# Two key blocks' weights of the first head pair made between the roots, with two table loads more

## The reference

```python
# _cdist: d2 = q2[..., :, None] + k2[..., None, :] - 2.0 * qk;  sqrt(max(d2, 0))
P = layernorm(x) @ W_in + b_in            # 16 heads x (Q, K, V, G), 64 wide each
W = jnp.power(EPS + _cdist(Q, K), -P_POW)  # EPS 1e-4, P_POW 2
W = W / (EPS + jnp.sum(W, axis=-1, keepdims=True))
A = jnp.einsum('hbts,hbse->hbte', W, V)
H = G * A                                  # then H @ W_out + b_out
```

## Time and profile before

| of the profiled execution | |
|---|---|
| its own time | 1395.16 us |
| span, first to last instruction | 1393.3 us |
| TensorE matmul busy | 1254.6 us (90%) |
| VectorE busy | 1129.7 us (81%) |
| ScalarE busy | 1034.0 us (74%) |
| GpSimd busy | 678.8 us (49%) |
| start, to the first distances of pair 1 | 74.4 us |
| granted TensorE clock, mean | 0.96 of full |

### The profile page before, as it was taken

One profiled execution on the slowest core, in us unless ns is written; L12 is line 12 of the kernel. 1 busy time (PEld: TensorE's weight loads), 2 busy tenths in 40 slices (PEclk: granted clock), 3 DMA queues, 4 the chain that ended last, 5 costly groups with the idle time before them and its releaser, 6 DMA issues.

```text
span 1393.3 us, 23237 instructions
## 1 busy us (share of the span) xinstructions
PE 1254.6 (90%) x7501; PEld 857.2 (62%) x7501; DVE 1129.7 (81%) x1563; ACT 1034.0 (74%) x835; POOL 678.8 (49%) x484
## 2 busy tenths in 40 slices
PE   5899999999999999999999893799998399999995
PEld 3545545554554555455455451688887299999994
DVE  6988988988898898889889765488887787787782
ACT  1599999999999999999999990233333157667662
POOL 5356566656656655665664415233332135445432
PEclk9899999999999999999999986899999599999998
DMA  5000000000000000000000104322222024443523
GB/s 164 4 16 17 18 28 15 30 15 30 15 15 30 15 30 16 25 20 15 30 8 15 29 1 129 123 69 68 68 77 76 23 83 115 100 104 53 151 34 83
DMA packets 69213, 68.06 MB, mean 49 GB/s; under 512 B 6816, under 2 KB 61344, under 8 KB 69152
## 3 DMA queue, kind: packets, MB, share of 16 engines
q1 hardware_dynamic: 61504, 57.19, 12.9%
q0 software_dynamic: 7680, 10.49, 4.5%
HBM read 49.32 MB, written 20.45 MB: 50 GB/s over the span
## 4 chain that ended last, share of the span: by engine, by line
PE 50%; ACT 19%; issue 15%; DVE 12%; DMA 2%; POOL 1%; DVEq 0%; POOLq 0%; ACTq 0%; SPq 0%
ACT wts L1598 12%; PE ps_s L577 8%; PE ps_s L847 8%; PE ps_o L880 6%; PE ps_o L593 6%; PE ps_o L666 4%; ACT wts L1600 4%; PE ps_p L488 4%; DVE wts L1061 4%; PE ps_p L847 3%; PE ps_s L699 2%; PE ps_s L727 2%; ACT L1595 1%; PE ps_o L684 1%; ACT rinv L1580 1%
## 5 line engine op out<-in xcount | busy, mean ns | idle before, releaser
L1061 DVE TENSOR_SCALAR wts<-ps_s,k 128x1024 f32<-128x1024 f32 x240 | 297.0, 1279 | 55.9 <-PE ps_s L577 52.6
L1797 POOL TENSOR_TENSOR v_aug<-v_aug,wts 128x1024 f32<-128x1024 f32 x96 | 232.6, 2423 | 224.2 <-DVE v_aug L1050 223.8
L593 PE MATMUL ps_o<-wts,head_rows 128*64 128x512 f32 x1024 | 247.9, 607 | 6.3 <-ACT wts L1600 6.3
L1592 ACT ACTIVATE wts<-wts 128x4096 f32<-128x4096 f32 (+1 forms) x80 | 230.1, 2932 | 22.8 <-DVE wts L1069 19.7
L1598 ACT ACTIVATE wts<-wts,eps_d 128x2048 f32<-128x2048 f32 (+1 forms) x96 | 246.0, 2562 | 0.2
L1600 ACT ACTIVATE wts<-wts 128x2048 f32<-128x2048 f32 (+1 forms) x96 | 238.4, 2484 | 3.1
L577 PE MATMUL ps_s<-q_hi,k_hi 64*128 64x512 f32 x512 | 123.1, 473 | 33.5 <-DVE wts L1061 17.8
L593 PEld LDWEIGHTS ps_o<-wts,head_rows 128*64 128x64 f32 x1024 | 62.8, 136 | 129.9 <-issue 116.0
L1050 DVE TENSOR_TENSOR v_aug<-v_aug,wts 128x1024 f32<-128x1024 f32 x96 | 126.6, 1319 | 6.6 <-ACT wts L1600 6.1
L1889 POOL DMA_INDIRECT acc<-norms,tok_put x40 | 63.9, 1598 | 106.2 <-ACT norms L1709 100.1
L577 PEld LDWEIGHTS ps_s<-q_hi,k_hi 64*128 64x128 f32 x512 | 49.4, 185 | 102.9 <-DVE wts L1061 62.5
(11 more groups left out here) (280 smaller groups left out, 3104.0 us busy)
## 6 DMA issues: line engine op xcount, KB each, us to landing
wts<-in_w SPq DMA_DIRECT2D x16, 704.0 KB, 5.7
raw<-in_w_in SPq DMA_DIRECT2D x64, 128.0 KB, 2.3
h_t<-o_step SPq DMA_DIRECT2D x16, 512.0 KB, 2.7
head_rows<-h_t SPq DMA_DIRECT2D x16, 512.0 KB, 4.3
wts<-in_w SPq DMA_DIRECT2D x8, 640.0 KB, 7.7
wts<-in_x SPq DMA_DIRECT2D x2, 1024.0 KB, 6.3
wts<-in_x SPq DMA_DIRECT2D x1, 2048.0 KB, 9.1
y_rows<-qk_sq SPq DMA_DIRECT2D x16, 128.0 KB, 1.7
```

What stands on the lines that cost most here:

```text
L593: mm = pe.matmul(ps_o[r, t], v_pair[:, b, r], wts[:, h, b, t], start=b == 0, stop=b == SB - 1)
L1061: dve.tensor_scalar(wts[:, h, b, :], ps_s[:, h, :], k2[:, 2 * b + h:2 * b + h + 1], 0.0, ALU.add, ALU.max).then_inc(S_.max_ok, 1)
L1592: act.activation(chunk(start, end), chunk(start, end), ACT.Sqrt).then_inc(S_.sqrt_ok, 1)
L1797: pool.tensor_tensor(acc_w[:, 0], acc_w[:, 0], wts[:, 0, b], ALU.add).then_inc(S_.add_ok, 1)
```

## The change

ScalarE's start of pair 0 is written out as `first_pair`: after the root of blocks 0 and 1 and images 4 and 5 it loads the table set of logarithm and exponential, makes the weights of block 0 and of block 1, loads the table set of the roots again, and goes on with images 6 and 7, all other roots, a third load and the weights of the other blocks. `roots` and `weights` are cut into `root` and `weight`, of which the loop's `pair` issues the same instructions in the same order as before. No other engine's program is changed.

```diff
-            def roots(n):
+            def root(n, start, end):
+                act.wait_ge(S_.max_ok, NB * n + 2 * end)
+                act.activation(chunk(start, end), chunk(start, end), ACT.Sqrt).then_inc(S_.sqrt_ok, 1)
+
+            def weight(n, c):
+                start, end = LOGS[c]
+                act.wait_ge(S_.sqrt_ok, len(ROOTS) * n + parts_until(ROOTS, end - 1))
+                act.activation(chunk(start, end), chunk(start, end), ACT.Ln, bias=eps_d[:, 0:1]).then_inc(S_.ln_ok, 1)
+                act.wait_ge(S_.ln_ok, len(LOGS) * n + c + 1)
+                act.activation(chunk(start, end), chunk(start, end), ACT.Exp, scale=-2.0).then_inc(S_.w_ok, 1)
+
+            def first_pair():
+                root(0, *ROOTS[0])
+                turned_high(4)
+                turned_high(5)
+                act.preload_act_table_set("natural_log_exp_and_others")
+                weight(0, 0)
+                weight(0, 1)
+                act.preload_act_table_set("sqrt_and_others")
+                turned_high(6)
+                turned_high(7)
+                for start, end in ROOTS[1:]:
+                    root(0, start, end)
+                act.preload_act_table_set("natural_log_exp_and_others")
+                for c in range(2, len(LOGS)):
+                    weight(0, c)
+
+            def pair(n):
                 for start, end in ROOTS:
-                    if isinstance(n, int) and start in (2, 4):
-                        turned_high(start + 2)
-                        turned_high(start + 3)
-                    act.wait_ge(S_.max_ok, NB * n + 2 * end)
-                    act.activation(chunk(start, end), chunk(start, end), ACT.Sqrt).then_inc(S_.sqrt_ok, 1)
...
-            roots(0)
-            weights(0, True)
+            first_pair()
             with act.Fori(1, PAIRS) as p:
-                roots(p)
-                weights(p, False)
+                pair(p)
```

More of the change, by code:

```diff
@@ L1584, in rows_inverse @@
                 act.activation(rinv[:], rinv[:], ACT.Exp, scale=-1.0).then_inc(S_.r_ok, 1)
-            def roots(n):
-                for start, end in ROOTS:
-                    if isinstance(n, int) and start in (2, 4):
-                        turned_high(start + 2)
-                        turned_high(start + 3)
-                    act.wait_ge(S_.max_ok, NB * n + 2 * end)
-                    act.activation(chunk(start, end), chunk(start, end), ACT.Sqrt).then_inc(S_.sqrt_ok, 1)
-            def weights(n, first):
-                act.preload_act_table_set("natural_log_exp_and_others")
[L1596 to L1601, removed]
+            def root(n, start, end):
+                act.wait_ge(S_.max_ok, NB * n + 2 * end)
+                act.activation(chunk(start, end), chunk(start, end), ACT.Sqrt).then_inc(S_.sqrt_ok, 1)
@@ L1602, in weights @@
+            def pair(n):
+                for start, end in ROOTS:
+                    root(n, start, end)
+                act.preload_act_table_set("natural_log_exp_and_others")
+                for c in range(len(LOGS)):
+                    weight(n, c)
+                    if c == 1:
                         rows_log(n - 1)
-                    if c == 3 and not first:
+                    if c == 3:
                         rows_inverse(n - 1)
-            roots(0)
-            weights(0, True)
+            first_pair()
```

## The result

| | runs | median us | lowest to highest |
|---|---|---|---|
| kernel before | 4 | 1394.01 | 1392.13 to 1396.33 |
| changed kernel | 4 | 1403.18 | 1399.51 to 1405.37 |

The ratio is 1.0057, 95% interval 1.0039 to 1.0075: 5.4 to 10.5 us slower. The profiled execution of the changed kernel is its fastest, 1399.51 us with a span of 1397.7.

A forecast was written before the change was run, and what follows sets the result against it. The prediction took the start to be bound by a chain of VectorE and TensorE, without ScalarE. A 5.7 us delay of VectorE plus 1.6 us of clock gave +7.3 us: 1392.4 + 7.3 = 1399.7 us, range 1395.5 to 1403.5.

The forecast's parts named there:

- Nothing on offer: Start, to 112.4 us: the chain runs through VectorE and TensorE alone, so filling ScalarE's idle time gains nothing.
- ScalarE's sum: ScalarE, pair 0: loads and weights put image 6 at 58.8 in place of 52.31, VectorE's turned_low(6) 5.7 us late.
- list of signs: Expected in the profile after: two more loads, image 6 at 58.8, VectorE's wait about 5.6 us, TensorE's gap 6 us.
- The gap: TensorE ahead of block 6's distances: 6.0 us without work, then half clock from 62 to 67 or 68.
- The clock's cost of 1.6 us: Behind TensorE's gap, up to guard 7: half clock adds 1.4 to 1.8 us, taken as 1.6, ends 0 and 2.5.
- the shift: VectorE from turned_low(6) on: starts at 59.4 in place of 53.68, everything behind it 5.7 us later.
- I leave that out of the sum: Projection of G(0): half clock in both kernels; if it kept the clock, copy_g(0) would lose a 0.6 us wait, not counted.
- Rigid behind pair 1: After pair 1's last guard: all that follows moves by the same amount, unless ScalarE is late there; turns of 48.97 us.
- Total: Whole kernel: 5.7 + 1.6 = +7.3 us, 1399.7 us against the median, 0.52% slower.

The follow-up runs named there:

- images_first: Changed kernel with the same two blocks' weights and two table loads moved behind the root of blocks 2 and 3 and images 6 and 7; 1394.78 us, ratio 1.0004.
- copies: Changed kernel with four same-size ScalarE copies where the early logs and exponentials stood, those weights made with the rest behind the roots; 1403.06 us, ratio 1.0052.
- loads_only: Changed kernel with the two table loads left between the roots but all weights made behind the roots as before; 1394.67 us, ratio 0.9998.
- after_late: Changed kernel with one more VectorE copy (128x1024) ahead of split_low(0) near the start; 1403.79 us, ratio 1.0061 against the kernel before.
- warm: Changed kernel with 24 extra matmuls, results overwritten, in TensorE's gap between the distances of blocks 5 and 6; 1398.13 us, ratio 1.0033.
- one_block: Changed kernel with only block 0's weights between the roots, block 1's made with the rest; 1397.87 us, ratio 1.0021.
- before_late: Kernel before with one more VectorE copy (128x1024) ahead of split_low(0) near the start; 1394.67 us, ratio 1.0000.
- the second series: The changed kernel run again without any edit (same_again), beside other kernels; 1404.0 us, ratio 1.0070 against the kernel before.
- low_late: Changed kernel with VectorE's turned_low(6) and (7) behind guard 6 in place of guard 4, ScalarE untouched; 1393.97 us, ratio 0.9997.
- both_warm: The kernel of both with 13 extra matmuls, results overwritten, in TensorE's gap between values(0, 0) and distances(1, 0); 1392.97 us, ratio 0.9995.
- early_k: Kernel before with VectorE's copy_k(1) ahead of guard 7 in place of behind it; 1394.72 us, ratio 1.0002.
- both: Kernel before with the edits of images_first and early_k: early weights behind images 6 and 7, copy_k(1) ahead of guard 7; 1394.36 us, ratio 0.9994.

## Why the prediction came out as it did

1. *Nothing on offer* on the chain: right. images_first gains 0.0 us at the last root, copies loses nothing by making the weights last.
2. *ScalarE's sum*: right. Loads at 47.47 and 56.58, image 6 at 57.87, each 0.9 us sooner than forecast as is all of the start; the wait of 5.69 us against 5.7 (5.6 in the list of signs). loads_only confirms 1.3 us for a switch. By the Trainium skill's drain ("ScalarE: Activation LUTs", "What ACT_TABLE_LOAD costs"), 1.38 us with each of two switches, the wait would by estimate have been 8.4 us; it was 5.69, no run here shows the drain, and the measurement decides.
3. *The gap*: 6.20 us against 6.0, and half clock behind it, right.
4. *The clock's cost of 1.6 us*: the term that was mis-sized. In the profile of the changed kernel guard 7 ended 1.3 us later than by the shift alone, but the projection of G(0), which I had said runs at half clock in both, began at full clock and gave 0.6 back (the part "I leave that out of the sum"): 0.7 us net. In copies it is 1.8 us net, in after_late 2.4 against the kernel before. By the ratios 8.0 - 5.7 = 2.3 and 9.8 - 5.7 = 4.1 us stand beside the shift, where I had 1.6; and warm is 5.9 us faster by the medians and only 0.6 at the last root of the profiles. Nor does the length of TensorE's pause ahead of the projection of G(0) say how it comes out: it was 3.31 to 3.33 us in the kernel before, images_first, loads_only, copies and warm, where the projection began at half clock, and in the changed kernel, one_block, before_late and after_late, where it began at full.
5. *Rigid behind pair 1*: right up to 800 us (table load of the last pair at 805.75 against 800.33), and so in every profile of this document: that load comes 687.8 to 688.0 us after the last root of pair 1. Behind it, it isn't: from that load to the end it is 591.9 to 595.7 us. There the kernel has a stage of its own chance, which the prediction left out; it is the last section's.
6. *Total*: forecast +7.3, measured +8.0 by the ratio (5.4 to 10.5), +9.8 in the second series (7.8 to 11.8). Of the 3.5 us between 1399.7 and 1403.18, 1.65 are the base: the three runs shown had a median of 1392.36, four of them 1394.01, and 15 to 29 runs of later series 1394.4 to 1394.6. The median lies only 0.3 us inside the upper end of the range, 1403.5, and the second series' 1404.0 beyond it. Direction and mechanism were right; that the number lay inside is in part luck.

What stays open is which part of the start or of the later stages holds the rest of what warm wins. The mean granted clock of the changed kernel's executions is 0.952 to 0.957 and warm's 0.958 to 0.962; no profile of an execution near the median was taken for either. The times of all executions say this much. The 91 executions of the kernel before in the four later series take 1392.7 us on average at a mean granted clock of 0.961 and 1397.3 at 0.954. Against a straight line through them, that is, at equal clock, the changed kernel's nine executions lie 5.9 us higher, those of copies 5.8, of after_late 6.1 and of warm 6.0; those of low_late and images_first lie within 0.3 us of it and both_warm's 1.0 us under it. So about the shift of 5.7 us is in all four alike, and what warm wins goes with the clock. This is a correlation and no experiment: the mean counts the clock of idle time too and doesn't say in which stage it was lost, and one_block lies 3.2 us above the line with a wait of 1.8 us.

## What to carry to other kernels

Idle time of an engine is not free room when something it does afterwards is awaited by a busier engine: before filling it, look at what is queued behind the filling, and date that against its consumer. Work moved forward is worth nothing unless its result is waited for; here the same move had no effect, cost 8 us, or took away a wait of 5.2 us (of TensorE in early_k), according to the order of a few lines on ScalarE or VectorE. A delay that leaves TensorE without matmuls for some us can cost its clock on top, and when a chain is shortened, the idle time that this opens can take half of the gain back (1.5 us left of 2.9 at pair 1's last root in both). And a gain in the profile of the start is not yet one in the time: both_warm's 2.9 us weren't found there.

## What the runs showed of the hardware

The granted clock also fell while TensorE was at work without a gap. The context stage ahead of the cross attention issues 80 small matmuls (L479) in one go. In the chain of waits of the kernel before, and then of copies:

```profile
807.00 12.20 PE ps_s L479 x80
```

```profile
814.71 15.80 PE ps_s L479 x80
```

And the stretches of the two, clock in the last column but two:

```profile
805.00:808.00 3.00, 2.98 (x27) 3.00 (x28) 0.00 (x0) 2.97 (x3) 0.00 (x0) 1.00 0.02 5
808.00:812.00 4.00, 4.00 (x37) 4.00 (x37) 2.51 (x3) 4.00 (x3) 0.00 (x0) 0.93 0.00 0
812.00:816.00 4.00, 4.00 (x21) 4.00 (x20) 0.00 (x0) 3.97 (x3) 0.00 (x0) 0.50 0.00 0
```

```profile
813.00:816.00 3.00, 3.00 (x26) 3.00 (x25) 0.00 (x0) 2.97 (x3) 0.00 (x0) 0.87 0.03 5
816.00:820.00 4.00, 4.00 (x20) 4.00 (x20) 2.51 (x3) 3.98 (x3) 0.00 (x0) 0.50 0.00 0
```

PE is busy throughout; its last pause before, of 0.73 us, ended at 805.02 and 812.73. By the mean clocks, an estimate, the clock falls to 0.50 some 4.4 us after the first of these matmuls in the kernel before and 0.5 us after it in copies; the stage takes 15.80 us in place of 12.20 (15.73 in images_first, 12.2 to 14.0 in the other profiles). This is 3.6 us of scatter by a stage that no edit here touches. In 11 or 12 runs it leaves an interval of 2.5 to 3.3 us, in which an edit worth 1.5 us in the trace, as both, isn't told from none. What decides when the clock falls there was not tested.

A VectorE difference of 128x896 took 2.78 us in the kernel before, where it began 0.09 us behind a GpSimd square of 128x1024:

```profile
64.78 2.78 DVE L1000 TENSOR_TENSOR o_step<-norms 128x896 f32<-128x896 f32 x1
```

```profile
64.69 1.93 POOL L1788 TENSOR_TENSOR k_sq<-norms 128x1024 f32<-128x1024 f32 x1 [12.77 <-DVE norms L995]
```

It ended 0.94 us after the square's end. In early_k (63.96, above) it took 1.08 us, where the square was over by 63.26 and GpSimd was at two operations of 128x256. That the square delayed it fits both and wasn't tested by itself.
